# Attention scores that stay in PSUM and go through their softmax in two halves of four heads

## The reference, cut to what matters

```
q, k = rms(q) * w, rms(k) * w                    # 8 query heads, 2 key heads, 64 wide
scores = einsum('bhqd,bhkd->bhqk', q, k) * 64 ** -0.5
scores = where(tril(256 x 256), scores, -inf)
attn_w = softmax(scores)                          # row maximum, exp, sum, divide
attn_out = einsum('bhqk,bhkd->bhqd', attn_w, v)
out = (attn_out + x @ W_VR per head) @ W_O
h = h + out
```

## Time and profile before

| | us |
|---|---|
| median of three runs | 2038.62 |
| the profiled execution's own time | 2039.54 |
| its span (first to last instruction) | 2037.8 |
| attention, first score to last addition | 297.7 to 525.0 |
| PE busy, whole span | 1829.7 (90%) |
| DVE busy, whole span | 1773.0 (87%) |
| ACT busy, whole span | 1452.1 (71%) |
| POOL busy, whole span | 681.8 (33%) |

### The profile page before, as it was taken

How to read it: one execution, slowest core, us unless ns; L and a number is a source line. 1 busy time by engine, 2 the same in 40 slices (tenths; PEclk the granted TensorE clock), 3 DMA queues, 4 the chain that set the end, 5 groups by cost and what they waited for, 6 DMA issues and landing times.

```text
span 2037.8 us, 29060 instructions
## 1 busy us (share of the span) xinstructions
PE 1829.7 (90%) x8486; PEld 1452.8 (71%) x8486; DVE 1773.0 (87%) x2326; ACT 1452.1 (71%) x2566; POOL 681.8 (33%) x439
## 2 busy tenths in 40 slices
PE   6455558999668999999999999999999999999998
PEld 4333335666446888888888888778888888888887
DVE  8435548887587999999999999989999999999997
ACT  2135547888226888888888888778888888888886
POOL 4250005665112333333333333323333333333330
PEclk9967769999658999999999999999999999999999
DMA  7410000000122333333333323323333333333331
GB/s 211 140 42 1 1 0 1 0 0 1 29 96 85 115 118 129 122 110 129 123 109 129 126 105 129 128 80 127 129 109 122 129 110 122 129 114 118 129 116 49
DMA packets 105257, 191.47 MB, mean 94 GB/s; under 512 B 13558, under 2 KB 86246, under 8 KB 88550
## 3 DMA queue, kind: packets, MB, share of 16 engines
q1 hardware_dynamic: 103166, 186.77, 26.5%
q0 software_dynamic: 2048, 4.20, 0.7%
HBM read 179.40 MB, written 11.53 MB: 94 GB/s over the span
## 4 chain that ended last, share of the span: by engine, by line
PE 69%; DVE 0%; issue 0%; ACT 0%; DVEq 0%; ACTq 0%
PE f_ps_h L1850 11%; PE f_ps_h L1851 11%; PE f_ps_h L1852 11%; PE f_ps_y L1861 11%; PE f_ps_y L1863 11%; PE f_ps_y L1862 11%; PE f_ps_y L1876 0%; DVE s_lo L1806 0%; DVE scaled L1800 0%; PE f_ps_h L1887 0%; ACT act_out L1761 0%; DVE h L1824 0%; ACT y_t L1785 0%; DVEq L1682 0%; PE f_ps_h L1832 0%
## 5 line engine op out<-in xcount | busy, mean ns | idle before, releaser
L1761 ACT ACTIVATE act_out<-f_ps_h,b_t 128x512 f32<-128x512 f32 x1024 | 649.5, 686 | 257.4 <-PE f_ps_h L1852 257.4
L1800 DVE TENSOR_TENSOR scaled<-act_out,c_row 128x1024 f32<-128x1024 f32 x512 | 752.1, 1469 | 43.3 <-ACT act_out L1761 42.7
L1806 DVE TENSOR_TENSOR s_lo<-scaled,s_hi 128x1024 fp32r<-128x1024 f32 x512 | 672.2, 1313 | 0.1
L1769 ACT ACTIVATE s_hi<-scaled 128x1024 fp32r<-128x1024 f32 x512 | 542.1, 1059 | 2.3 <-DVE scaled L1800 1.5
L1664 POOL CAST w_hi<-w_raw 128x512 fp32r<-128x512 f32 x128 | 200.6, 1567 | 910.0 <-PE f_ps_y L1863 898.2
L1850 PE MATMUL f_ps_h<-x_hi,w_hi 128*128 x1024 | 399.8, 390 | 2.2 <-DVE h L1824 1.5
L1861 PE MATMUL f_ps_y<-s_hi,w_hi 128*128 128x512 f32 x1024 | 398.7, 389 | 3.0 <-DVE s_lo L1806 3.0
L1851 PE MATMUL f_ps_h<-x_lo,w_hi 128*128 x1024 | 399.3, 390 | 0.0
L1852 PE MATMUL f_ps_h<-x_hi,w_lo 128*128 x1024 | 399.2, 390 | 0.0
L1863 PE MATMUL f_ps_y<-s_hi,w_lo 128*128 128x512 f32 x1024 | 398.4, 389 | 0.0
L1862 PE MATMUL f_ps_y<-s_lo,w_hi 128*128 128x512 f32 x1024 | 398.4, 389 | 0.0
(11 more groups left out here) (219 smaller groups left out, 1581.1 us busy)
## 6 DMA issues: line engine op xcount, KB each, us to landing
c_row<-comb_rows SPq DMA_DIRECT2D x128, 1024.0 KB, 4.8
w_raw<-in_w SPq DMA_DIRECT2D x256, 128.0 KB, 4.2
by_slot<-b_zeros SPq DMA_DIRECT2D x1, 3072.0 KB, 13.6
b_gauss_s<-by_slot SPq DMA_DIRECT2D x12, 256.0 KB, 5.8
mixed_rows<-b_mixed SPq DMA_DIRECT2D x12, 256.0 KB, 2.6
out<-h SPq DMA_DIRECT2D x8, 256.0 KB, 4.6
cent<-in_centers SPq DMA_DIRECT2D x1, 1536.0 KB, 6.9
neg_prec<-in_logvar SPq DMA_DIRECT2D x1, 1536.0 KB, 10.8
```

The lines of the kernel that those rows point to most:

```text
L1761: last = act.activation(act_out[:, r % 2, c, :], ps_h[:, r % 2, c, :], ACT.Gelu, bias=b1_t[:, c, bass.ds(e, 1)])
L1769: act.activation(s_hi[:, r % RING], scaled[:, r % RING], ACT.Copy).then_inc(hi_ready, 1)
L1800: dve.tensor_tensor(scaled[:, r % RING], act_out[:, r % 2], c_row[:, k, g * GT:(g + 1) * GT].unsqueeze(1).broadcast_to([P, HC, GT]), ALU.m ...
L1806: dve.tensor_tensor(s_lo[:, r % RING], scaled[:, r % RING], s_hi[:, r % RING].bitcast(F32), ALU.subtract).then_inc(lo_ready, 1)
```

## The change

The scores stay in PSUM until the exps. The eight heads are split into two halves: half 0 is heads 0, 4, 1, 5 in the first two banks of `ps_s`, half 1 is heads 2, 6, 3, 7 in the last two (`heads_of`, `half_of`, `place`). Each half is scored, masked in place in PSUM, reduced to its maxima from PSUM, and its exps read PSUM and write `sm`. `copy_far` is gone. `score` of a half waits for the exps of the same half of the unit before (`exp_done`, now counted twice a unit) instead of `masked`. The order of the steps changes on three engines: PE scores half 0 before `turn_k` and half 1 after `project_out`; DVE does mask and maximum of half 0 behind `copy_q`, then `invert` (now of unit u-1), `add_y`, `statistics`, then mask and maximum of half 1; ACT does the exps of half 1 of unit u-1 behind the first `copy_p`, then the second `copy_p`, `copy_k`, and the exps of half 0 of unit u. POOL's order stays.

```diff
--- before.py
+++ after.py
@@ -1085,7 +1085,7 @@
 def attend(nc, h, ident, causal, w_out, k_scale, qk, v_all, rms, mv):
 
     UNITS = 2 * BATCH
-    FIRST_EXPS = 5
+    HALF = HEADS // 2
     with ExitStack() as ctx:
         def sb(name, shape, dt=F32):
             return ctx.enter_context(nc.sbuf_tensor(name, shape, dt))
@@ -1098,7 +1098,7 @@
         q_t = sb("q_t", [P, 2, GROUP, P])
         k_t = sb("k_t", [P, 2, SEQ])
         sm = sb("sm", [P, 4, HEADS, SEQ])
-        neg_max = sb("neg_max", [P, 4, HEADS])
+        neg_max = sb("neg_max", [P, 2, KV, KV])
         rowsum = sb("rowsum", [P, 4, HEADS])
         rinv = sb("rinv", [P, 4, HEADS])
         p_t = sb("p_t", [P, 2, HEADS, P])
@@ -1137,6 +1137,15 @@
             whole = u // 2 if isinstance(u, int) else (u - r % 2) // 2
             return whole * 3 + r % 2
 
+        def heads_of(a):
+            return [g * GROUP + a * KV + b for b in range(KV) for g in range(KV)]
+
+        def half_of(a):
+            return ps_s[:, a * HALF:(a + 1) * HALF, :].rearrange("p (g b) k -> p g b k", g=KV)
+
+        def place(n):
+            return n % GROUP // KV * HALF + n // GROUP * KV + n % KV
+
         def all_steps(eng, step):
 
             for u in range(8):
@@ -1161,16 +1170,15 @@
                     act.wait_ge(p_turned, blocks_before(u, r) + k + 1)
                     act.activation(p_t[:, k], ps_p[:], ACT.Copy).then_inc(p_copied, 1)
 
-            def exps(u, r, heads_of):
+            def exps(u, r, a):
                 if in_range(u, UNITS):
                     keys = (r % 2 + 1) * P
-                    if 0 in heads_of:
-                        act.wait_ge(max_ready, u + 1)
-                    for n in heads_of:
-                        last = act.activation(sm[:, r, n, 0:keys], sm[:, r, n, 0:keys], ACT.Exp,
-                                              bias=neg_max[:, r, n:n + 1], accum_out=rowsum[:, r, n:n + 1])
-                    if HEADS - 1 in heads_of:
-                        last.then_inc(exp_done, 1)
+                    act.wait_ge(max_ready, 2 * u + a + 1)
+                    for n in heads_of(a):
+                        last = act.activation(sm[:, r, n, 0:keys], ps_s[:, place(n), 0:keys], ACT.Exp,
+                                              bias=neg_max[:, a, n // GROUP, n % 2:n % 2 + 1],
+                                              accum_out=rowsum[:, r, n:n + 1])
+                    last.then_inc(exp_done, 1)
 
             def copy_mv(u):
                 if in_range(u, UNITS):
@@ -1181,11 +1189,11 @@
                 if r == 1:
                     copy_mv(u - 9)
                 copy_p(u - 4, r, 0)
-                copy_k(u + 1, (r + 1) % 4)
-                exps(u - 2, (r - 2) % 4, range(FIRST_EXPS, HEADS))
+                exps(u - 1, (r - 1) % 4, 1)
                 if r % 2:
                     copy_p(u - 4, r, 1)
-                exps(u - 1, (r - 1) % 4, range(0, FIRST_EXPS))
+                copy_k(u + 1, (r + 1) % 4)
+                exps(u, r, 0)
 
             copy_k(0, 0)
             all_steps(act, step)
@@ -1240,31 +1248,24 @@
                     dve.wait_ge(y_ready, u + 1)
                     dve.tensor_tensor(h[:, u, :], h[:, u, :], ps_qy[:, 0, :], ALU.add).then_inc(y_added, 1)
 
-            def copy_far(u, r):
-
-                if in_range(u, UNITS) and r % 2:
-                    dve.wait_ge(scored, u + 1)
-                    dve.tensor_copy(sm[:, r, :, 0:P], ps_s[:, :, 0:P])
-
-            def mask(u, r):
+            def mask(u, r, a):
                 if in_range(u, UNITS):
                     q = r % 2
-                    dve.wait_ge(scored, u + 1)
-                    if q:
-                        after(dve, p_turned, blocks_before(u - 4, r) + q + 1)
-                    dve.tensor_tensor(sm[:, r, :, q * P:(q + 1) * P], ps_s[:, :, q * P:(q + 1) * P],
-                                      causal[:].unsqueeze(1).broadcast_to([P, HEADS, P]), ALU.add
-                                      ).then_inc(masked, 1)
-
-            def maximum(u, r):
+                    dve.wait_ge(scored, 2 * u + a + 1)
+                    own = half_of(a)[:, :, :, q * P:(q + 1) * P]
+                    dve.tensor_tensor(own, own, causal[:].unsqueeze(1).unsqueeze(1).broadcast_to([P, KV, KV, P]),
+                                      ALU.add).then_inc(masked, 1)
+
+            def maximum(u, r, a):
                 if in_range(u, UNITS):
-                    dve.wait_ge(masked, u + 1)
-                    dve.tensor_reduce(neg_max[:, r, :], sm[:, r, :, 0:(r % 2 + 1) * P], AX.X, ALU.max, negate=True
-                                      ).then_inc(max_ready, 1)
+                    after(dve, exp_done, 2 * u + a - 1)
+                    dve.wait_ge(masked, 2 * u + a + 1)
+                    dve.tensor_reduce(neg_max[:, a], half_of(a)[:, :, :, 0:(r % 2 + 1) * P], AX.X, ALU.max,
+                                      negate=True).then_inc(max_ready, 1)
 
             def invert(u, r):
                 if in_range(u, UNITS):
-                    dve.wait_ge(exp_done, u + 1)
+                    dve.wait_ge(exp_done, 2 * u + 2)
                     dve.reciprocal(rinv[:, r, :], rowsum[:, r, :]).then_inc(rinv_ready, 1)
 
             def statistics(u, slot):
@@ -1281,12 +1282,13 @@
             def step(u, r):
                 copy_o(u - 5)
                 copy_q(u, r)
-                maximum(u - 1, (r - 1) % 4)
-                copy_far(u, r)
-                mask(u, r)
-                invert(u - 2, (r - 2) % 4)
+                mask(u, r, 0)
+                maximum(u, r, 0)
+                invert(u - 1, (r - 1) % 4)
                 add_y(u - 5)
                 statistics(u - 5, (r - 5) % 4)
+                mask(u, r, 1)
+                maximum(u, r, 1)
 
             all_steps(dve, step)
 
@@ -1344,27 +1346,29 @@
                                              start=(k == 0), stop=(k == q))
                     last.then_inc(mixed, 1)
 
-            def score(u, r):
+            def score(u, r, a):
 
                 if in_range(u, UNITS):
                     q, s = r % 2, r // 2 % 2
-                    pe.wait_ge(q_copied, u + 1)
-                    pe.wait_ge(k_copied, u + 1)
-                    after(pe, masked, u)
-                    for n in (n for pair in range(GROUP) for n in (pair, pair + GROUP)):
+                    if a == 0:
+                        pe.wait_ge(q_copied, u + 1)
+                        pe.wait_ge(k_copied, u + 1)
+                    after(pe, exp_done, 2 * u + a - 1)
+                    for n in heads_of(a):
                         at = slice(n // GROUP * HD, (n // GROUP + 1) * HD)
-                        last = pe.matmul(ps_s[:, n, 0:(q + 1) * P], q_t[at, q, n % GROUP, :],
+                        last = pe.matmul(ps_s[:, place(n), 0:(q + 1) * P], q_t[at, q, n % GROUP, :],
                                          k_t[at, s, 0:(q + 1) * P], start=True, stop=True)
                     last.then_inc(scored, 1)
 
             def step(u, r):
                 v = u - 4
                 turn_p(v, r, 0)
+                score(u, r, 0)
                 turn_k(u + 1, (r + 1) % 4)
-                score(u, r)
                 if r % 2:
                     turn_p(v, r, 1)
                 project_out(u - 5)
+                score(u, r, 1)
                 mix(v, r)
                 turn_q(u + 1, (r + 1) % 4)
```

## The result

The changed kernel takes 2054.16 us (median of four, 2053.30 to 2055.58) against 2039.07 for the kernel before in the same number of runs: a ratio of 1.0075, 95% interval [1.0058, 1.0093], 15 us slower. 2053 was forecast, in a range of 2043 to 2064. One execution of a later run, e6, took 2758.62 us at a mean granted clock of 0.65, and is left out of that run's ratio.

The account below looks back on a forecast made before the run. Attention was taken as bound by a 13.17 us ring per pair, 6.04 POOL and 7.13 PE's queue. 2039.54 + 14.6 (13 pairs) + 2 (start) - 2.5 (end) = 2053.6, or 2053 as median; range 2043 to 2064.

Parts of the forecast that it names:

- the ring: Mid-attention chain of waits from turn_q to turn_q, now also through ACT and DVE: 14.29 us a pair against 13.17.
- rival B: DVE's in-place PSUM masks dearer: 1.21 instead of 0.68 us, exps at the upper end, 2061 us in all; chance 0.13.
- step 3: DVE, after the exps of half 1: from invert to what follows statistics 1.02 us, ahead of the second half's mask.
- Both holes of PE: PE standing about 1.1 us before the even unit's second-half scores (exps), 0.75 before the odd unit's first half (copy_q).
- the forecast margin: POOL's 6.04 us from turn_q to turn_p fit in the 6.61 now there, so POOL no longer binds.
- rival C: POOL stays the bound at 6.04 us, about 0.3 less in a pair: faster, 2034 us; chance 0.07.
- Rival D: The pieces overlap more than laid: 13.6 to 13.9 us a pair, 2042 to 2046 us in all; chance 0.14.
- E: Rival: PE's granted clock falls for a quarter of the attention stage, 27 us more, 2080 us; chance 0.03.
- the 0.06 for faster: Chance given to a whole-kernel time under 2034.5 us, beside 0.06 for same and 0.88 for slower.
- The start: First pairs of attention at the lower clock: some +0.9 us a pair for a little over two pairs, +2.
- my 7.1: Start of attention, odd unit's scores to the next unit's: 7.1 us reckoned for the 6.83 before the change.
- the -2.5: End of attention, exps a step earlier: 9.6 us from mix to mix instead of 12.08, so 2.5 us saved.

Follow-up runs that it names:

- e6: Changed kernel with DVE's maximum of half 1 moved from the end of its own step to behind copy_q in the next; ratio 1.0046 to the kernel before.
- e1: Changed kernel with ACT's exps of half 1 of unit u-1 ahead of the first copy_p instead of behind it; ratio 1.0036 to the kernel before.
- e9: Changed kernel with the four exps of half 0 of every unit done twice, first into a spare tile; ratio 1.0103 to the kernel before.
- e10: Changed kernel with the four exps of half 1 of every unit done twice, first into a spare tile; ratio 1.0359 to the kernel before.
- e3: Changed kernel with DVE's invert of unit u-2, as before the change, instead of unit u-1; ratio 1.0058 to the kernel before.
- e5: Changed kernel with POOL's copy_v and norm_p moved ahead of norm_qk; ratio 1.0073 to the kernel before.
- e2: Changed kernel's order and halves, but scores go to SBUF, with a far copy for each half of an odd unit; ratio 1.0156 to the kernel before.
- e4: Kernel before the change with POOL's copy_v and norm_p moved ahead of norm_qk; ratio 0.9988 to the unedited kernel before.

## Why the prediction was right

Step by step, by the prediction's own numbers:

1. `turn_q` to `turn_p` 0.49, to `copy_p` 1.08, to the exps 0.92: 2.49 (2.51).
2. Exps of half 1 every 0.45, and 0.16 to the wake-up: 4.45 (4.50). e1, e9 and e10 show this piece to be in the ring. They follow each other closer than from SBUF (0.45 for 0.49), as the scaled copy's row had suggested.
3. `invert` to the mask 1.09 (1.02). e3 shows it to be in the ring.
4. Mask in place 0.70 (0.68), so rival B's upper end, 1.21, was far off. Mask to maximum 0.80 where I had 0.71, a dependent instruction's wait of 0.10, not 0.03. This and the 1.09 of step 3 are the two terms of the ring that I had too small; three of the others came 0.02 to 0.04 shorter than laid, which hid a part of it in the sum. Scores at 8.36 (8.29).
5. PE's queue 6.02 (6.00). In all 14.38 (14.29). e6 shows the maximum and `copy_q` to be in the ring.

Both holes of PE came where they were put, 1.00 and 0.70 for 1.1 and 0.75. POOL dropped out with the forecast margin, and e5 confirms it; rival C, with POOL still the bound, fell with it. Rival D would have needed 13.9 or less. The clock stayed at 1.00 (E), though in e10 it fell behind ten of twelve holes that were 1.9 us longer. One slip in the chances changed nothing: of the 0.06 for faster only half of C, 0.035, is accounted for.

The maximum of 1024 elements took 1.225 us from PSUM and 1.208 from SBUF, 0.017 more, and against e2's 1.220, which has the same shape, 0.005 more. By the Trainium skill, VectorE: DVE Perf Modes, section "The TRN2 errata — SBUF-src ops pay a fixed extra latency per instruction", the fixed part is 120 cycles from PSUM and 58 from SBUF, by estimate 0.065 us more. The trace does not agree, and the measurement decides.

The ends were less well laid. The start cost 3.2, not 2: two masks and two maxima ahead of `copy_q` made each of the first pairs 1.2 to 1.5 longer (10.77 for 9.57, 12.33 for 10.82), not 0.9. The growth lies in the even step, where from scores to scores it took 5.00 (294.46 to 299.46) for 4.01 before, +1.0 and not my 0.6. The first odd step took 6.84 for 6.83; my 7.1 for it was a wrong sum, its parts make 6.8.

The steady part has 12 pairs between these marks; the thirteenth I had counted is in the end's -0.7, for which my numbers say 1.1 - 2.5 = -1.4. It is the -2.5 that was mis-sized: from the `mix` at 513.95 to that at 524.24 it took 10.29 for 12.08, so -1.8. I had laid the second `copy_p` at 6.3 behind the first `mix`; it started at 6.9 (520.88), because ACT first had to wait for the statistics that it copies once in four steps, an instruction that my account of the end does not name:

```profile
520.77 0.21 ACT L1186 ACTIVATE mv<-a_mv_ring 128x8 f32<-128x8 f32 x1 [0.97 <-DVE a_mv_ring L1280]
```

Attention grew by 16.3, not 14.1: the start, the steady part and the end all missed to the same side. The 14.1 stood closer to the profiled executions' difference, 13.8, only because untouched stages were 2.6 shorter that time. So the mechanism and the ring's length were right on their merits, but part of the close agreement in the total, 2053 for 2054.16, is luck.

## What to carry to other kernels

When several in-order engines work on each other's results, look for the ring: follow one instruction through queues and semaphores until it comes back, one period later. Its length is the period, a change costs what it adds to the ring and gives what it takes from it until another chain of waits is the longer one (e1, e4), and busy shares say nothing: 3.2 us more work for ACT in each pair cost nothing in mid-attention, outside the ring. Smaller pieces with more hand-overs need their place in every queue chosen anew; where a piece queues behind an instruction that waits for another engine, that wait becomes its own.

## What was not expected of the hardware

Holes of 1.00 and 0.70 us in PE's work, in each 14.38 us, left the granted clock at 1.00. With a hole of 2.9 us in each 16.5 to 19.2 it came down to 0.86 in a stretch of 60 us: the matmuls behind ten of twelve such holes ran at the lower level (1.97 for 1.08), behind two they did not. So the doubling of half 1 made attention 59 us longer (305.0 against 245.9), where 2.1 us for each of some fifteen pairs would have been 32; the stage's start and end, which grew too, are in the 59.
